# The first layer's bf16 part rows laid out as 128 + 16, its last batch prepared a step earlier, and its first independent units moved between fills

## The reference

```python
a  = layer_norm(ctx) * gamma + beta          # 4 x 256 x 256
q  = (x @ Wq.T) * 16 ** -0.5                 # per head 256 x 16
k  = a @ Wk.T ;  v = a @ Wv.T
p  = softmax(q @ k.T + mask)                 # per batch and head 256 x 256
x += tanh(gate) * ((p @ v) @ Wo.T)
```

## Time and profile before

| what | value |
|---|---|
| median of 3 runs | 1302.26 us (1301.91 to 1302.64) |
| span of the profiled execution, first to last instruction | 1301.2 us |
| own time of the profiled execution | not listed besides its span |
| mean granted clock of TensorE in it | 0.970 |
| TensorE busy, share of the span | 94% |
| first layer in it | 0 to about 185 us |

### The profile page before, as it was taken

The page is one execution under the profiler, slowest core; times in us unless marked ns, Lnnn a source line. Parts: engine busy times, 40 slices in busy tenths (PEclk is TensorE's granted clock), DMA queues, the critical chain, the costliest instruction groups (busy, mean ns, idle before and its releaser), DMA issues.

```text
span 1301.2 us, 17916 instructions
## 1 busy us (share of the span) xinstructions
PE 1222.6 (94%) x6064; PEld 859.9 (66%) x6064; DVE 792.9 (61%) x2354; ACT 537.2 (41%) x1233; POOL 216.2 (17%) x429
## 2 busy tenths in 40 slices
PE   6789989999998879999998899999999999999998
PEld 4467655556464434444433788888888888888887
DVE  4445438778675157787875666666656666666530
ACT  3145343444444315545555343434333434343432
POOL 3023025242434020112101100000000000000000
PEclk9689799999999879999999999999999999999999
DMA  7434741110202455515426903030303030500000
GB/s 226 141 114 136 222 155 64 57 64 35 81 26 93 135 177 183 159 73 164 139 83 198 312 1 130 1 130 1 130 1 130 1 131 1 195 1 1 1 9 25
DMA packets 100650, 127.58 MB, mean 98 GB/s; under 512 B 6736, under 2 KB 78576, under 8 KB 98320
## 3 DMA queue, kind: packets, MB, share of 16 engines
q1 hardware_dynamic: 99936, 126.14, 29.6%
q10 hardware_dynamic: 624, 0.30, 0.1%
HBM read 79.33 MB, written 46.79 MB: 97 GB/s over the span
## 4 chain that ended last, share of the span: by engine, by line
PE 79%; DMA 6%; DVE 4%; SPq 3%; ACT 3%; POOL 2%; issue 2%; ACTq 0%; POOLq 0%; DVEq 0%
PE J L2464 8%; PE J L2484 8%; PE TT L2472 8%; PE TT L2448 4%; PE S L2438 4%; PE OO L2438 4%; PE OO L1091 4%; PE OO L1088 4%; PE J L324 2%; PE J L1357 2%; PE OO L2705 2%; PE J L1091 2%; PE S L1327 2%; PE S L648 2%; PE J L333 2%
## 5 line engine op out<-in xcount | busy, mean ns | idle before, releaser
L2542 ACT ACTIVATE PT<-TT 128x512 f32<-128x512 f32 x128 | 76.4, 597 | 279.9 <-PE TT L2448 279.9
L2577 POOL COPY On<-probs 128x8 f32<-128x8 f32 x128 | 29.2, 228 | 470.0 <-DVE probs L2612 440.7
L2623 DVE TENSOR_SCALAR QK<-J,cols 128x256 f32<-128x256 f32 x126 | 61.0, 484 | 68.5 <-PE J L2464 68.5
L2612 DVE TENSOR_SCALAR probs<-probs,inv 128x257 f32<-128x257 f32 x256 | 79.0, 351 | 4.5
L2448 PE MATMUL TT<-ident,probs 128*128 128x128 f32 x512 | 76.9, 273 | 2.6 <-DVE probs L2612 2.6
L2448 PEld LDWEIGHTS TT<-ident,probs 128*128 128x128 f32 x512 | 63.8, 141 | 16.4 <-DVE probs L2612 3.8
L2618 DVE COPY km<-TT 128x256 f32<-128x256 f32 x128 | 54.2, 423 | 30.6 <-PE TT L2472 30.3
L1091 PE MATMUL OO<-ctxT,weights_a 128*128 128x512 f32 x136 | 66.4, 610 | 6.2 <-SPq L308 3.5
L1088 PE MATMUL OO<-weights_a,ctxT 128*128 128x512 f32 x136 | 65.9, 607 | 6.6 <-ACT weights_a L1102 3.4
L2331 DVE TENSOR_TENSOR_SCAN early<-km,early 128x256 f32<-128x256 f32 x64 | 64.3, 1044 | 10.9 <-ACT early L2102 10.1
L2484 PE MATMUL J<-early,km 128*128 128x256 f32 x256 | 65.8, 379 | 0.3 <-DVE km L2618 0.3
(11 more groups left out here) (414 smaller groups left out, 2711.7 us busy)
## 6 DMA issues: line engine op xcount, KB each, us to landing
wide_keys<-weights_a SPq DMA_DIRECT2D x64, 256.0 KB, 2.1
wide_values<-weights_a SPq DMA_DIRECT2D x56, 256.0 KB, 2.0
query_parts<-weights_a SPq DMA_DIRECT2D x48, 192.0 KB, 2.9
weights_a<-wide_keys SPq DMA_DIRECT2D x16, 512.0 KB, 7.3
weights_a<-wide_values SPq DMA_DIRECT2D x16, 512.0 KB, 8.4
early<-wide_keys SPq DMA_DIRECT2D x16, 512.0 KB, 7.8
early<-wide_values SPq DMA_DIRECT2D x16, 512.0 KB, 9.1
weights_a<-key_parts SPq DMA_DIRECT2D x16, 288.0 KB
```

Source lines behind the costliest of these rows:

```text
L2542: act.activation(PT[:, n % 2, :], T0[:, :], ACT.Copy).then_inc(pt3_ready, 1)
L2612: ins = dve.tensor_scalar(P_[n % 2][:, qt, :], P_[n % 2][:, qt, :], inv[:, qt, n % 32:n % 32 + 1], None, ALU.mult)
```

## The change

The part rows are laid out as 16 features x 3 x 3 with the first 128 in slot 0 and the last 16 (third part by third part) in slot 1; the rows of maxima follow these 16, so slot 1 has 16 rows for a fill and 19 for a transposed score. The query parts are written to DRAM once per batch (two DMAs, not six). Rows are read with four DMAs for keys and four for queries per step: 48, 48, 32 and 16 rows, each with the 16 features outermost on the DRAM side. Batch 3 is prepared in step 1, not step 2, with its statistics and root a step earlier; the values of batch 1 are projected at the end of step 0. The rows of steps 2 and 3 are issued ahead of the loop, without the wait for maxima; those of steps 4 to 7 at chunk 2 of steps 1 to 4. The key parts of batch 1 are written before the rows of step 1 are read. One unit remains ahead of the first fill; the other seven follow the last fill of step 0 and the first six of step 1, one each, and ScalarE copies each a chunk later.

```diff
-        ROWS0 = PARTS * PARTS * HALF0
+        FEATS0 = 2 * HALF0
+        REST0 = FEATS0
+        TOPS0 = [PARTS, PARTS, PARTS - 1]
+        ROWS0 = [0, PARTS * FEATS0, 2 * PARTS * FEATS0]
...
+        FIRST_AT = [-7, -6, -5, -4, -3, -2, -1]
...
         def prepared(n):
 
-            return n // 2 + 2 if n >= 0 and n % 2 == 0 and n // 2 + 2 < B else None
+            return n + 2 if 0 <= n < B - 2 else None
...
         def keep_queries0(sp, b):
             sp.wait_ge(queries0_split, b + 1)
             for s in range(2):
-                for c in range(PARTS):
-                    sp.dma_start(query_parts0[b, s, :, c].rearrange("a p n -> p a n"),
-                                 parts0["q"][:, :, s * S:(s + 1) * S]).then_inc(query0_kept, 16)
+                sp.dma_start(query_parts0[b, :, s].rearrange("a p n -> p a n"),
+                             parts0["q"][:, :, s * S:(s + 1) * S]).then_inc(query0_kept, 16)
...
+        def feature_rows(parts, first):
+            return parts.rearrange("c s (d h) n -> (s d) c (h n)", d=HALF0)[:, :, first * S:(first + HEADS_AT) * S]
...
-            for s in range(2):
-                sp.dma_start(k_rows0[m % 4][0:ROWS0, s, :, :],
-                             key_parts0[b, s].rearrange("c (d h) n -> (c d) (h n)", d=HALF0)[:, here]
-                             .unsqueeze(0).to_broadcast([PARTS, PARTS * HALF0, n_here]))\
+            keys = feature_rows(key_parts0[b], first)
+            for a, top in enumerate(TOPS0):
+                sp.dma_start(k_rows0[m % 4][ROWS0[a]:ROWS0[a] + top * FEATS0, 0, :, :], keys[:, 0:top, :])\
                     .then_inc(rows0_landed[m % 4], 16)
+            sp.dma_start(k_rows0[m % 4][0:REST0, 1, :, :], keys[:, 2, :]).then_inc(rows0_landed[m % 4], 16)
...
+            queries = feature_rows(query_parts0[b], first)
+            for a, top in enumerate(TOPS0):
+                sp.dma_start(q_rows0[m % 4][ROWS0[a]:ROWS0[a] + top * FEATS0, 0, :, :],
+                             queries[:, a:a + 1, :].to_broadcast([FEATS0, top, HEADS_AT * S]))\
                     .then_inc(rows0_landed[m % 4], 16)
+            sp.dma_start(q_rows0[m % 4][0:REST0, 1, :, :], queries[:, 2, :]).then_inc(rows0_landed[m % 4], 16)
...
             spread0(sp, 0)
+            keep_keys0(sp, 1)
             spread0(sp, 1)
-            keep_keys0(sp, 1)
             keep_queries0(sp, 1)
+            spread0(sp, 2)
+            spread0(sp, 3)
             for at in range(-LEAD0, LAST0):
                 n, i = at // CHUNKS0, at % CHUNKS0
-                b = n // 2
-                if i == 5 and 0 <= n + 1 < STEPS0:
-                    if n < 0:
-                        sp.wait_ge(max0_rows_ready, n + 2)
-                        spread0(sp, n + 3)
-                if at == 1:
-                    spread0(sp, 3)
...
+                if prepared(n) is not None and i == 4:
+                    keep_keys0(sp, prepared(n))
+                if prepared(n - 1) is not None and i == 1:
+                    keep_queries0(sp, prepared(n - 1))
+                if 1 <= n <= STEPS0 - 4 and i == 2:
+                    spread0(sp, n + 3)
...
+                    tops = (P, REST0)
                     for qt in range(TQ):
                         for s in range(2):
                             mm = pe.matmul((S0, S1)[n % 2][:, qt * S:(qt + 1) * S],
-                                           q_rows0[m % 4][0:ROWS0, s, f, qt * P:(qt + 1) * P],
-                                           k_rows0[m % 4][0:ROWS0, s, f, :], start=(s == 0), stop=(s == 1))
+                                           q_rows0[m % 4][0:tops[s], s, f, qt * P:(qt + 1) * P],
+                                           k_rows0[m % 4][0:tops[s], s, f, :], start=(s == 0), stop=(s == 1))
...
-                            top = ROWS0 + (PARTS if s == 1 else 0)
+                            top = (P, REST0 + PARTS)[s]
...
-                for u in range(FIRST - 1):
+                def first_unit(u):
                     if u == 1:
                         pe.wait_ge(values0_ready, 1)
                     if u >= 2:
                         pe.wait_ge(ahead_copied, u - 1)
                     project_ahead(pe, (J1, O0)[u % 2], u)
+
+                first_unit(0)
...
-                    if i == 7 and n >= 0 and n % 2 == 1 and b + 1 < B:
+                    if i == 7 and n == 0:
+                        pe.wait_ge(h0_ready, 2)
+                        values(1, J0)
+                    if i == 7 and n >= 3 and n % 2 == 1 and b + 1 < B:
                         pe.wait_ge(ot0_ready, n)
                         values(b + 1, J0)
...
-                    if at == -1:
-                        u = FIRST + at
-                        pe.wait_ge(ahead_copied, u - 1)
-                        project_ahead(pe, (J1, O0)[u % 2], u)
+                    if at in FIRST_AT:
+                        first_unit(1 + FIRST_AT.index(at))
...
-                    if n in (-1, 1) and i == 0:
-                        root((n + 5) // 2 + 1)
+                    if n in (-1, 0) and i == 0:
+                        root(n + 4)
```

More of the change, by code:

```diff
@@ L550, in spread_keys0 @@
                 sp.wait_ge(st0_done, CHUNKS0 * (m - 3))
-            here = slice(first * S, (first + HEADS_AT) * S)
-            n_here = HEADS_AT * S
             sp.wait_ge(key0_kept, 16 * 2 * (b + 1))
-            for s in range(2):
-                sp.dma_start(k_rows0[m % 4][0:ROWS0, s, :, :],
-                             key_parts0[b, s].rearrange("c (d h) n -> (c d) (h n)", d=HALF0)[:, here]
-                             .unsqueeze(0).to_broadcast([PARTS, PARTS * HALF0, n_here]))\
+            keys = feature_rows(key_parts0[b], first)
+            for a, top in enumerate(TOPS0):
+                sp.dma_start(k_rows0[m % 4][ROWS0[a]:ROWS0[a] + top * FEATS0, 0, :, :], keys[:, 0:top, :])\
                     .then_inc(rows0_landed[m % 4], 16)
+            sp.dma_start(k_rows0[m % 4][0:REST0, 1, :, :], keys[:, 2, :]).then_inc(rows0_landed[m % 4], 16)
         def spread_queries0(sp, m):
             b, first = m // 2, m % 2 * HEADS_AT
[L563 to L567, removed]
+            sp.wait_ge(query0_kept, 16 * 2 * (b + 1))
+            queries = feature_rows(query_parts0[b], first)
+            for a, top in enumerate(TOPS0):
+                sp.dma_start(q_rows0[m % 4][ROWS0[a]:ROWS0[a] + top * FEATS0, 0, :, :],
+                             queries[:, a:a + 1, :].to_broadcast([FEATS0, top, HEADS_AT * S]))\
                     .then_inc(rows0_landed[m % 4], 16)
+            sp.dma_start(q_rows0[m % 4][0:REST0, 1, :, :], queries[:, 2, :]).then_inc(rows0_landed[m % 4], 16)
         def split0(eng, n, ready, done_sem, turn, step_sem, at):
@@ L602, in stacked0_sp @@
                     store_first(sp, i)
[L603 to L613, removed]
+                if prepared(n) is not None and i == 4:
[4 more added lines that the diff above has]
+                    spread0(sp, n + 3)
                 if n == 4 and i == 2:
                     sp.wait_ge(key0_kept, 16 * 2 * B)
-                    sp.wait_ge(query0_kept, 16 * 2 * PARTS * B)
+                    sp.wait_ge(query0_kept, 16 * 2 * B)
                     load_values()
@@ L750, in pe_program @@
                             pe.wait_ge(max0_rows_ready, n + 1)
+                            if prepared(n - 1) is not None:
+                                pe.wait_ge(queries0_ready, following)
                             flip_x(following, O1)
@@ L771, in pe_program @@
                         if n == 1:
-                            pe.wait_ge(h0_ready, 2)
+                            pe.wait_ge(values0_ready, 2)
+                        elif n == 2:
+                            pe.wait_ge(ot0_ready, 1)
                         elif n % 2 == 1:
@@ L871, in act_program @@
                 act.wait_ge(mask_ready, 4)
-                for u in range(FIRST - 1):
-                    copy_first(act, (J1, O0)[u % 2], u)
+                copy_first(act, (J1, O0)[0], 0)
                 for at in range(-LEAD0, LAST0):
                     n, i = at // CHUNKS0, at % CHUNKS0
-                    if at == 0:
-                        copy_first(act, (J1, O0)[(FIRST + at - 1) % 2], FIRST + at - 1)
+                    if at - 1 in FIRST_AT:
+                        u = 1 + FIRST_AT.index(at - 1)
+                        copy_first(act, (J1, O0)[u % 2], u)
                     if at >= 1:
@@ L1046, in dve_program @@
                         add_out(b - 1)
-                    if n >= 2 and n % 2 == 0 and i == 0:
+                    if n == 1 and i == 0:
+                        fetch_values(1, J0)
+                    if n >= 4 and n % 2 == 0 and i == 0:
                         fetch_values(b, J0)
-                    if n in (-1, 1):
+                    if n in (-1, 0):
                         if i == 0:
-                            statistics((n + 5) // 2)
+                            statistics(n + 3)
                         if i == 5:
```

(2 more changed lines are left out.)

12 lines of the change are left out of this document (6 added, 6 removed).

## The result

The changed kernel takes 1372.38 us (median of 4 runs, 1366.42 to 1385.3) against 1302.45 for the kernel before (four runs): 1.0541 of it, with a 95% interval of 1.0481 to 1.0600. The forecast was 1276. The profiled execution of the changed kernel is the longest of the four, 1385.3 us with a span of 1383.5.

A forecast was written before the change was run, and what follows sets the result against it. TensorE was taken as the busy engine, waiting on row DMAs and often at low clock after stops. Terms 6.4 + 5.3 + 4.2 + 10.7 = 26.6 us off 1301.2, with 1.06 added 1275.7, forecast 1276; range 1271 to 1288.

The forecast's parts named there:

- Rows as 128 + 16: Matmuls split into 128 and 16 rows: four still take 0.44 us, cost 0; upper bound 0.87 for four.
- The other side: Rival, chance 0.06: 128 and 16 row pairs lower the loop's clock, 1.2 us more per chunk; all 64 give 1353.
- terms 2 to 4: Loop gains: chunks 0 to 2, 5.3 us; step 1's stop, 4.2; the stop before step 6's rows, 10.7.
- The start: Before the loop: first step's rows there at 29 to 31 us, not 40.45; loop starts at 55.3, bounds 52.7 and 60.
- term 1: Start of the first layer's loop: it begins at 55.3 instead of 61.7, a gain of 6.4 us.
- Chunks 0 to 2: Loop's first chunks: 5.9 us in place of 11.2, with 0.6 of waits for ScalarE's copies; gain 5.3 us.
- term 3: Step 1, batch 3's preparation: earlier statistics and root remove TensorE's stop for GpSimd's maxima and the low clock after; 4.2 us.
- term 4: Step 6's rows, issued in step 3: 3.3 us of waiting and 7.4 of low clock go; gain 10.7 us.
- DMAs: Row loads and query writes: four of six writes go; new row DMAs use 16 engines, 4.1 us a step.
- slow rows: Rival, chance 0.07: new rows run at 77 GB/s, loop starts near 71, a gain of some 5, 1290 to 1300.
- a new stop: Rival, chance 0.20: GpSimd's maxima, a row or a copy is late in the loop; 4.2 to 10.7 us, 1280 to 1287.
- a late second layer: Rival, chance 0.05: the second layer's last load doesn't move, meeting waits until 171, 14 us of gain left: 1288.

The follow-up runs named there:

- the padded kernel: The changed kernel with slot 1 filled with zero rows to 96 (fills) and 99 (transposed scores): 1275.72 us, 0.9764 of before.
- units first: The changed kernel with slot 1 zero-padded to 96 rows and seven units in a row ahead of the first fill again: 1274.91 us, 0.9783 of before.
- old rows: The changed kernel with two slots of 72 rows and their DMAs as in the kernel before: 1301.78 us, 0.9981 of before.
- three-quarters kernel: The changed kernel with only the transposed scores' slots reordered to 128, 19, 19, 128, fills still alternating 128 and 16: 1313.93 us, one run.

## Why the prediction was wrong, point by point

**The step that failed** is *Rows as 128 + 16*: "four of them take 0.44", "So I cost this at 0", with 0.87 as the upper bound. It measured 0.85. The nearest row was looked for by columns and by type, and the bf16 matmuls of the second layer that it stood on are of one row count in a row; the earlier trace rows shows no matmul of 64 rows or fewer beside one of 128, which is the thing that is new. The Trainium skill's rule on changes of the mode, named above, speaks against this change; the prediction did not weigh it. The trace of before had a hint, too: transposed scores straight behind a weighted sum, whose weights are 128 x 32, took 0.55 and not 0.45, with no wait between:

```profile
75.95 1.00 PE J L679 x16
76.95 0.55 PE TT L663 x4
```

They take 0.55 there in the padded kernel as well (at 64.78); whether that is the same pause, no run tests. The upper bound, taken from the float32 projection for another reason, had the size. 114 groups in the loop (64 transposed scores, 50 fills) at 0.41 make 46.7 us, and taken up, that bound would have turned the sign.

**The clock.** The rival "The other side" had the place (the pairs let the clock fall inside the loop), a chance of 0.06, and a price of 1.2 us per low chunk. Its ground was a stretch of 72-row matmuls that stayed low after a stop; what came, at 117 us for one, was a fall with TensorE busy throughout. The argument against it, "the rows per pair are the same 144", did not bear on what was new: with the same rows, TensorE got through 5.9 matmuls per us and not 8.9. The loop's 203.6 us are 100.5 above the 103.1 that the forecast leaves it (123.3 − terms 2 to 4): 46.7 of pauses, and 53.8 that remain for the low clock and small waits. Checked from the other end: a mean of 0.64 between 1.00 and 0.50 is 72% of 203.6 us at the low level, 147 us, in which a group takes 1.29 in place of 0.85, a third of it lost: 50.

**The start.** Rows at 31.9 for "29 to 31", and a loop start of 62.84 for 55.3. The padded kernel starts at 54.94. The 7.9 us between the two are the eight fills (10.41 us against 7.2 from 31.94 to 39.13), six later fills (0.75 against 0.44), a first unit at the low clock (3.48 against 1.72) and five units of 1.91 against 1.72: 3.2 + 1.9 + 1.8 + 1.0 = 7.9. That VectorE's split would hold the third fill until 31.3 did not come true: it was done at 31.1 in the changed kernel and at 29.73 in the padded one, before the rows came. The rows were last.

**The remaining terms stand, as the padded kernel shows.** Its loop starts at 54.94 (term 1, 55.3) and its last projection ends at 160.8, against 158.4 forecast (185.0 − 26.6):

```profile
157.19 3.58 PE J L333 x8
...
160.79 0.75 DVE x_tok L1019
```

That projection ran at the low clock, 3.58 where it took 2.01 in the chain of before. Chunks 0 to 2 took 6.8 us (54.94 to 61.77) for 5.9: a wait of 1.1 for ScalarE's copies is longer than the 0.6 forecast. TensorE's wait for GpSimd's maxima fell from 3.1 us to 0.4 (term 3), and those for query rows from 5.1 to none (term 4). The time is 1275.72, the sum 1275.7. To the microsecond this is luck: the padded kernel's profiled execution took 1277.99, its layer ended 2.4 later than forecast, and the rest of the kernel was 0.8 shorter. How the gain splits is another matter: units first says that the order of units and fills in term 1 brought nothing, and old rows that without the DMAs the stops of terms 3 and 4 go but others come in their place, and the sum is nothing.

**DMAs.** The new rows ran at a share near 1, the writes were fewer, and no load held up the second layer: this step stands, and the rivals of slow rows, a new stop and a late second layer did not occur. The rule on the number of engines that the prediction took from the Trainium skill, page "DMA: Bandwidth & Descriptors", section "Why a DMA increments its semaphore by 16 and not by 1", gives 16 for these rows; the trace agrees, with the share of 0.94.

## What to carry to other kernels

When the contract rows of matmuls are split unevenly, look at each neighbour: a matmul of 64 rows or fewer next to one of more than 64 cost 0.10 us each way here, about the time of a 256-column bf16 matmul, while zero rows up to 96 cost nothing. Where the short ones can't be padded, put them next to each other. And read busy TensorE with care: 100% busy, with fewer matmuls per us than elsewhere at the same clock, was a run of pauses, and the fall of the clock that came with it doubled the loss. The fastest kernels here, the padded one and its twin with units first, are 1275 to 1276 us, 2.2 to 2.4% below before.

## What the runs showed of the hardware

- A change of contract rows from 128 to 64, 32 or 16, or back, took TensorE 0.10 us at 2.4 GHz (0.64, 0.75 and 0.85 us for two, three and four of them in a group of four bf16 matmuls that takes 0.44 without), and none from 128 to 67, 96 or 99. A change from 16 rows to f32 matmuls of 128 rows took more: 0.15 for four of 128 columns (0.59 against 0.44) and 0.19 for eight of 256 (1.92 against 1.73).
- Single matmuls in the profile hardly show it. In the listing by shape of the three-quarters kernel the 16-row fills take 278 ns on average and the padded kernel's 96-row ones 273; the pause is in the distance between starts:

```profile
L644 PE MATMUL S<-weights_a,early 16*128 16x256 bf16 x64 | 17.8, 278 | 0.0
```

```profile
L644 PE MATMUL S<-weights_a,early 96*128 96x256 bf16 x56 | 13.9, 273 | 0.0
```

- The granted clock fell to 1.2 GHz inside stretches in which TensorE was listed 100% busy. In both profiles of the changed kernel it first came back as eight f32 matmuls of a projection ended (3.41 us for them, then groups of 0.75 and 0.85), but not behind each of them: the clock stayed at 0.50 behind those at 166.0.

```profile
86.91 3.41 PE OO L324 x8
90.32 0.75 PE TT L659 x4
```

- Matmuls of 8 columns between others of more than 64 rows took 0.027 us each with four in a group (0.55 against 0.44); 16 of them in a group of four cost 0.40 (0.84 against 0.44).
